# One stage of a four-stream decoder kernel: chunk loads, order of the MLP's matmuls, value heads and row maximum changed together

## The reference

```python
scores = jnp.einsum('bhid,bhjd->bhij', q, k) * scale
kerple = -p * jnp.log1p(a * dist[None])
combined = jnp.concatenate([attn_t, kerple_t], axis=-1)         # 16 scores, 16 kerple values per (i, j)
hdn = jax.nn.gelu(jnp.dot(combined, w1) + b1, approximate=False) # w1 is 32 x 32
refined = jnp.dot(hdn, w2) + b2                                  # w2 is 32 x 16
scores = scores + kerple[None] + refined
scores = jnp.where(causal[None, None], scores, -jnp.inf)
weights = jax.nn.softmax(scores, axis=-1)
out = jnp.einsum('bhij,bhjd->bhid', weights, v)
```

## Time and profile before

| what | value |
|---|---|
| runs | 5373.63, 5384.91, 5383.06 us |
| the profiled execution | 5373.67 us |
| its span, first to last instruction | 5371.9 us |
| mean granted TensorE clock | 0.918 |
| PE / PEld / DVE / ACT busy in the span | 4611.2 / 2081.7 / 2563.6 / 1934.2 us |
| second half of A in the second round | 1478 to 1763.2 us |

### The profile page before, as it was taken

How to read it: one execution, slowest core, us unless ns; L and a number is a source line. 1 busy time by engine, 2 the same in 40 slices (tenths; PEclk the granted TensorE clock), 3 DMA queues, 4 the chain that set the end, 5 groups by cost and what they waited for, 6 DMA issues and landing times.

```text
span 5371.9 us, 51967 instructions
## 1 busy us (share of the span) xinstructions
PE 4611.2 (86%) x18614; PEld 2081.7 (39%) x18714; DVE 2563.6 (48%) x5396; ACT 1934.2 (36%) x3234; POOL 308.7 (6%) x299
## 2 busy tenths in 40 slices
PE   5897888899788778889978877888997887788999
PEld 2333334345434333434533423342453342334345
DVE  4455635542345563554234566365423546535632
ACT  5542432331554243333155333333315533323320
POOL 1000130000000013000000002300000000230000
PEclk9998978999899898899989988899998998889999
DMA  6744003312374400331237440032213734004121
GB/s 235 155 101 83 14 1 73 59 63 73 106 137 93 83 14 4 81 48 68 68 112 140 84 83 14 27 69 37 74 62 126 140 71 83 14 32 81 19 83 57
DMA packets 173150, 398.65 MB, mean 74 GB/s; under 512 B 16164, under 2 KB 93988, under 8 KB 161828
## 3 DMA queue, kind: packets, MB, share of 16 engines
q1 hardware_dynamic: 172872, 395.08, 31.3%
HBM read 315.33 MB, written 79.69 MB: 74 GB/s over the span
## 4 chain that ended last, share of the span: by engine, by line
PE 66%; DVE 16%; DMA 8%; ACT 4%; issue 3%; SPq 2%; another core or an unknown queue 1%; POOLq 0%; DVEq 0%; ACTq 0%
PE ps L1020 9%; PE ps L510 6%; PE ps L1278 5%; DVE mx L640 5%; PE ps L1288 5%; PE ps L493 5%; PE ps L1038 4%; PE ps L436 4%; PE ps L1313 3%; DMA a_cmb<-scores_kerple 3%; PE ps L780 3%; PE ps L762 3%; PE ps L332 2%; DMA qparts<-QP 2%; ACT a_rot L1353 2%
## 5 line engine op out<-in xcount | busy, mean ns | idle before, releaser
L640 DVE TENSOR_REDUCE mx<-ps 128x1 f32<-128x512 f32 (+3 forms) x1280 | 770.2, 645 | 537.0 <-PE ps L441 260.6
L584 ACT ACTIVATE PT<-ps 128x1024 f32<-128x1024 f32 (+3 forms) x640 | 604.7, 958 | 522.4 <-PE ps L498 287.6
L436 PE MATMUL ps<-KS,QS 96*128 96x512 bf16 (+3 forms) x1280 | 488.2, 404 | 195.2 <-DMA QS<-qparts 116.9
L1020 PE MATMUL ps<-xnT,f_w 128*128 128x512 f32 x1088 | 488.8, 593 | 0.0
L493 PE MATMUL ps<-QS,KS 99*128 99x512 bf16 (+2 forms) x1280 | 425.5, 377 | 9.0 <-ACT QS L574 6.2
L1278 PE MATMUL ps<-a_cmb,w1A 128*128 128x512 f32 (+1 forms) x704 | 370.2, 610 | 48.8 <-DMA a_cmb<-scores_kerple 48.1
L510 PE MATMUL ps<-PT,VP 128*32 128x512 f32 (+3 forms) x2560 | 380.7, 581 | 3.3
L332 PE MATMUL ps<-mneg,identb 128*128 128x512 bf16 x856 | 214.4, 409 | 141.9 <-issue 50.1
L1118 DVE TENSOR_TENSOR f_tm<-f_si,ps 128x512 f32<-128x512 f32 x128 | 88.0, 687 | 503.2 <-ACT f_si L1070 503.1
L436 PEld LDWEIGHTS ps<-KS,QS 96*128 96x128 bf16 x1280 | 130.1, 102 | 486.3 <-DVE mx L640 278.1
L1070 ACT ACTIVATE f_si<-ps 128x512 f32<-128x512 f32 x136 | 80.8, 597 | 607.6 <-PE ps L1033 588.5
(11 more groups left out here) (245 smaller groups left out, 6576.1 us busy)
## 6 DMA issues: line engine op xcount, KB each, us to landing
f_w<-in_wF SPq DMA_DIRECT2D x136, 384.0 KB, 3.0
a_cmb<-scores_kerple SPq DMA_DIRECT2D x64, 512.0 KB, 10.7
a_cmb<-scores_kerple SPq DMA_DIRECT2D x64, 384.0 KB, 11.1
VP<-in_v_unit SPq DMA_DIRECT2D x12, 2048.0 KB, 10.5
KS<-kparts SPq DMA_DIRECT2D x96, 256.0 KB, 9.6
QS<-qparts SPq DMA_DIRECT2D x144, 128.0 KB, 5.2
scores_kerple<-a_Ss SPq DMA_DIRECT2D x16, 1024.0 KB, 6.2
a_cmb<-scores_kerple SPq DMA_DIRECT2D x64, 256.0 KB, 8.1
```

Of the source, the lines that this page charges most:

```text
L436: last = nc.tensor.matmul(o, m["QS"][0:KR, h, i * P:(i + 1) * P], m["KS"][0:KR, h, f:f + w], start=True, stop=plain)
L584: nc.scalar.activation(m["PT"][:, mp % 2, j % 2, :, 0:w], ps[:, b0:b0 + 2, 0:w], ACT.Exp, scale=HD ** -0.5).then_inc(g("exp"), 1)
L640: nc.vector.tensor_reduce(m["mx"][:, h % 2, i, f // BANK:f // BANK + 1], ps[:, k % 2, 0:w], AX.X, ALU.max, negate=True).then_inc(g("slot_f ...
L1020: last = nc.tensor.matmul(ps[:, 2 * v + e % 2, :], m["w"][:, e % NRING, (2 * v + k) * P:(2 * v + k + 1) * P], xnT[:, k, :], start=(k == 0) ...
```

## The change

Five edits, all in the first attention:

1. `load(c)`: the four `a_cmb` DMAs become two, one for each half f, each writing all 128 partitions. The source of each has the row group as its outermost dimension (4), then the 32 values.
2. The waits for the stores of row tiles 1, 2 and 3 stood before the first load of each tile (chunks 4, 8, 12); now all three stand before `load(1)`, which is before the mid-stage barrier.
3. TensorE's order: instead of up, down, up, down it is two ups, then the two downs of the pair before, one in each half of the array's columns.
4. `weighted`: for each pair of heads and each key tile j, first the even head (lower half of the columns), then the odd head, instead of all j of one head after another.
5. VectorE: the addition of the table and the row maximum are one operation per row, `tensor_tensor_reduce`, instead of an addition per row and one `tensor_reduce` per chunk.

```diff
@@ -1202,11 +1204,10 @@
 
             def load(c):
                 i, r, R, L = chunk(c)
-                rows = sk[i].rearrange("r (f g q) j -> g r f (q j)", f=2, g=4)
+                rows = sk[i].rearrange("r (f g q) j -> f g r (q j)", f=2, g=4)
                 part = slice(r * L, (r + R) * L)
-                for u in range(4):
-                    sp.dma_start(M2["cmb"][32 * u:32 * u + 32, c % 2, 
-                                 :, 0:R * L], rows[u, :, :, part]).then_inc(g(f"cmb{c % 2}"), 16)
+                for f in range(2):
+                    sp.dma_start(M2["cmb"][:, c % 2, f, 0:R * L], rows[f, :, :, part]).then_inc(g(f"cmb{c % 2}"), 16)
                 if c >= 4:
                     sp.wait_ge(g("tr"), TURNS_TO[c - 3])
                 rows = sk[i][0:AH].rearrange("h (g q) j -> g h (q j)", g=8)
@@ -1223,8 +1224,9 @@
                 sp.dma_start(sk[i][4 * hq:4 * hq + 4].rearrange("h p j -> p h j"),
                              M1["Ss"][:, 4 * sum(TRI_L[:i]):4 * sum(TRI_L[:i + 1])].rearrange("p (h l) -> p h l", h=4)).then_inc(g(f"out{i}"), 16)
             for c in range(1, NCHUNK):
-                if CHUNKS[c][1] == 0:
-                    sp.wait_ge(g(f"out{CHUNKS[c][0]}"), 4 * 16)
+                if c == 1:
+                    for i in range(1, NI):
+                        sp.wait_ge(g(f"out{i}"), 4 * 16)
                 if c >= 2:
                     sp.wait_ge(g("w1"), UNITS_TO[c - 1])
                 load(c)
@@ -1271,7 +1273,7 @@
                 c, f, q = A_UNITS[k]
                 i, _, _, L = chunk(c)
                 if k == UNITS_TO[c]:
-                    pe.wait_ge(g(f"cmb{c % 2}"), 16 * 4 * (c // 2 + 1))
+                    pe.wait_ge(g(f"cmb{c % 2}"), 16 * 2 * (c // 2 + 1))
                 if k >= 3:
                     pe.wait_ge(g("gelu"), k - 2)
                 R = SA_R[i]
@@ -1305,9 +1307,8 @@
 
             def weighted(i):
                 pe.wait_ge(g("pt_up"), TURNS_TO[TILE_END[i] + 1])
-                for h in range(AH):
-                    r, t = AW * (h % 2), h // 2
-                    for j in range(i + 1):
+                for t, j, e in itertools.product(range(AH // 2), range(i + 1), range(2)):
+                        h, r = 2 * t + e, AW * e
                         rhs = m["PT"][:, j, :, :].rearrange("p q (g h) -> p h g q", h=AH)[:, h]
                         o = ps[r:r + AW, 4 + t // 4, (t % 4) * P:(t % 4 + 1) * P].rearrange("p (g q) -> p g q", g=8)
                         last = nc.tensor.matmul(o, m["V"][:, j, h * AW:(h + 1) * AW], rhs, start=(j == 0), stop=(j == i), tile_position=(0, r))
@@ -1327,10 +1328,12 @@
             for s in range(NCHUNK + 3):
                 c = s - 2
                 if s < NCHUNK:
-                    for k in range(UNITS_TO[s], UNITS_TO[s + 1]):
-                        if k + 2 < len(A_UNITS):
-                            up(k + 2)
+                    for k in range(UNITS_TO[s], UNITS_TO[s + 1], 2):
+                        for e in (k + 2, k + 3):
+                            if e < len(A_UNITS):
+                                up(e)
                         down(k)
+                        down(k + 1)
                 if 0 <= c < NCHUNK:
                     turn(c, 0)
                 if s - 3 in TILE_END:
@@ -1427,12 +1430,12 @@
                         for q in range(q0, q0 + R):
                             row = m["fin"][:, slot, q * L:(q + 1) * L]
                             t0 = BACK - i * P - (r + q)
-                            last = nc.vector.tensor_tensor(row, row, biasA[:, t0:t0 + L], ALU.add)
+                            last = nc.vector.tensor_tensor_reduce(row, row, biasA[:, t0:t0 + L], 1.0, NEG, ALU.add, ALU.max,
+                                                                  m["nm"][:, slot, q:q + 1])
                         ch.link(last)
                     if s >= 2:
                         turned(s - 2, 1)
                     nm = m["nm"][:, slot, 0:CR]
-                    ch.link(nc.vector.tensor_reduce(nm, m["fin"][:, slot, 0:CR * L].rearrange("p (q l) -> p q l", q=CR), AX.X, ALU.max))
                     nc.vector.tensor_scalar(nm, nm, -1.0, None, ALU.mult).then_inc(g("negm"), 1)
                 if NCHUNK <= s < NCHUNK + 2:
                     turned(s - 2, 0)
```

More of the change, by code:

```diff
@@ L8 @@
+import itertools
 import numpy as np
```

## The result

| | before | after |
|---|---|---|
| median, four executions each | 5383.99 us | 5648.60 us |
| from to | 5373.63 to 5388.82 | 5634.32 to 5676.92 |
| after / before | | 1.050 [1.046, 1.054] |
| the profiled execution | 5373.67 | 5676.92 |
| mean granted TensorE clock | 0.918 | 0.880 |

The change makes the kernel 265 us slower. The forecast was +862 (6245); the direction and the place are right, the size is 3.3 times too large.

What follows compares the result with a forecast made beforehand. The prediction took DMA on four engines to bound stage A's second half: +216 us a round, +864 for four. 5373.7 + 864 = 6237.7; with the median 9.4 above the profiled execution, 6245, own range 5950 to 6400.

Steps and rivals of the forecast that it cites:

- Four engines: New a_cmb loads, source outermost dimension 4, run on four engines, assumed among a_fin's eight; 0.74 at 12.5 to 19 GB/s each.
- Bounds of the rate: Per engine in the new loads: 14.9 GB/s chosen, between 13.1 (+273 us a round) and 26.4 (+112).
- the term of 430 us for the loads: Second half of stage A: after chunk 0's load, 25.56 MB on four engines at 59.5 GB/s take 429.6 us a round.
- Rival 1: Four engines load undisturbed at 26.4 GB/s each: +112 us a round, 5495 us; chance 0.13.
- the signs that the prediction had named: Second half of A: DMA share 0.25 to 0.3, 50 to 70 GB/s, TensorE busy under half, clock below 0.93.
- No gap opens in between: Second half of A: each chunk's load is issued while the previous one still arrives, so loading never pauses.
- The chunk of 44 us: A row tile 3 chunk, 2.62 MB on four engines, takes 44 us to load; TensorE needs about 18.
- The tail and the clock: From the last landing to stage B: 64 us, plus 8 us (0 to 35) for a lower TensorE clock.
- Edit 2: Moved store waits delay chunk 1's load and the barrier: some 9 us a round, bounds 0 to 15.
- Edit 3: Second down of a pair is free: 40.6 us a round if TensorE sets the pace, here only 4.
- Edit 5: Combined addition and maximum on VectorE: 0 taken; saving 2.3 us or costing 1.3 in each of the last two chunks.
- Rival 2: New loads still spread over sixteen engines, TensorE sets the pace: -45 us a round, 5203 us; chance 0.09.

Runs made afterwards that it cites:

- e3_rmajor: After with the a_cmb partitions ordered value first and w1A's rows permuted to match, so the source's outermost dimension is 32: 5197.25 us.
- e8_two: After with each a_cmb load cut into two of 64 partitions, source outermost dimension 2: 6360.03 us.
- e10_eight: After with a_cmb partitions value first and each load cut into four by value, 32 partitions a load, source outermost dimension 8: 5312.37 us.
- e9_few_fin: After with most of a_fin not loaded from chunk 5 on and other data for chunks 1 to 4, so scores are wrong: 5590.64 us.
- e1_loads: Before with only the new two a_cmb loads per chunk and the store waits moved ahead of load(1): 5731.84 us.
- e7_waits: Before with only the store waits moved ahead of load(1) and the barrier: 5403.30 us.
- e5_max: Before with only addition and row maximum made one operation: 5367.29 us.
- e2_rest: After with the old four a_cmb loads per chunk, all other edits kept: 5361.75 us.
- e4_pairs: Before with only TensorE's order changed to two ups, then two downs: 5328.46 us.
- e11_four: After with a_cmb partitions value first and each load cut into eight by value, 16 partitions a load, source outermost dimension 4: 5720.69 us.

## Why the prediction was right in kind and wrong in size

**Four engines: right**, shown by the shares and by e3_rmajor and e8_two. That they are among `a_fin`'s eight is right too (0.52 with both in flight).

**The step that failed is "Bounds of the rate", and with it the term of 430 us for the loads.** It took 14.9 GB/s an engine "of the load with the most similar source and target". That row shows eight engines at little more than half of what eight moved in e10_eight, and I carried its rate to four. My own sentence beside it, that 119 GB/s for both eight and sixteen engines is a limit of what is shared, should have moved the choice towards 26.4. In after, windows of 3 us from 1552.77 on add up to 30.7 MB by the last `a_cmb` landing at 1853.7, in 301 us: 102 GB/s. Five sixths of it are the four's by the prediction's own bytes (26.2 of 31.5 MB), 85 GB/s or 21 each. With 85 for 59.5 GB/s the 25.56 MB take 301 us and not 430: -129 us a round, and that alone turns +216 into +87; measured are +75 and 6.7 at the barrier in the second round, and 66 a round in the medians. Rival 1's rate (26.4) errs nearly as far to the other side of 21 as 14.9 does, but in time it is closer: 5495 against 5649, since time goes with the inverse. The windows show three kinds of stretches below 26.4: starts at 59 to 67 GB/s (the partitions are the likely cause, not shown), `a_fin` beside (0.52 to 0.53 with 112 to 134 GB/s, 13 to 16 each; e9_few_fin), and ends and gaps in which two engines or none are at work. Of the signs that the prediction had named, the quarter share and the lower clock (0.80 over the half) came, but so did the sign against it, 90 GB/s and more at a quarter share (106), and TensorE was busy for 63% of the half, not for under half of it.

**"No gap opens in between" failed too**, though the total hides it. The chain of waits from 1700 to 1915 us of after names the loads for 40.8% of the time and TensorE's own rows for most of the rest; three of its pieces (start, us, what):

```profile
1701.59 8.59 PE ps L1314 x64
...
1716.83 40.01 DMA a_cmb<-scores_kerple
...
1805.90 47.79 DMA a_cmb<-scores_kerple
```

In e9_few_fin no byte moves from 1704.77 to 1708.77, just behind `weighted`. With two buffers a load waits for TensorE's ups, so TensorE's time is not free in this kernel. That this is why edits 3 to 5 took 83 us off e1_loads, 21 a round where I had 4, is argued, not shown.

**The chunk of 44 us** was near for row tile 3 (40.0 and 47.8 us above, each including what is queued ahead), and wrong for the sum: in row tile 2 two loads follow each other by 23 us (issued at 1662.94 and 1685.94) where 1.97 MB at 59.5 GB/s were to take 33.

**The tail and the clock.** From the last landing to stage B I had 64 + 8 us; it took 59.7 (1853.73 to 1913.47). The clock did fall to 0.50 while TensorE stood waiting for a load. But at the last landing TensorE had worked since 1830.82 with few pauses, on `weighted` of row tile 2 and the matmuls of chunk 14, and the clock stood at 1.00. It fell later, to between 0.50 and 0.84 from 1876.77 to 1891.77, and was 0.91 in the mean of the piece, where the same piece of before had 0.82 (1695.90 to 1763.22). So the 8 us for a lower clock are the second mis-sized term: nothing of it came.

**Edit 2: right.** I had 9 us a round within 0 to 15; the barrier comes 6.7 us later in round two and e7_waits measures 5.6 a round.

**Edit 3: right for TensorE.** Two downs now take 1.01 us together. TensorE of after in row tile 3 (start, us, line, form, count):

```profile
1765.31 0.64 PE L1290 MATMUL ps<-a_hid,w2A 128*64 128x512 f32 x1
1765.31 0.64 PE L1290 MATMUL ps<-xn,w2A 128*64 128x512 f32 x1
1765.79 0.59 PE L1290 MATMUL ps<-a_hid,w2A 128*64 128x512 f32 x1
1765.79 0.59 PE L1290 MATMUL ps<-xn,w2A 128*64 128x512 f32 x1
1766.31 1.98 PE L1280 MATMUL ps<-a_cmb,w1A 128*128 128x512 f32 x4
```

The pairs start in the same 10 ns. Two ups and two downs take 2.92 us (1765.31 to 1768.23) and took 4.12, 1.2 saved where I had 1.0. In after the loads hid most of it. With 16 engines on 128 partitions it can reach the time (e3_rmajor, 5197), though no run has those loads without edit 3.

**Edit 4: right** at 0. `weighted` of row tile 3, every matmul of it alternating, takes

```profile
1890.79 17.02 PE L1314 MATMUL ps<-a_PT,a_V 128*64 128x128 f32 x128 [0.78 <-DVE a_PT L1412]
```

where it took 16.57.

**Edit 5: right at 0 here**, inside its bounds: VectorE's new operation costs what the addition did, and its short partner 0.08 us and not 0.2.

```profile
1801.91 0.69 DVE L1433 CUSTOM_DVE_ANT_0 a_fin<-a_fin,biasA 128x512 f32<-128x512 f32 x1
1802.53 0.08 DVE L1433 DVE_READ_ACCUMULATOR2_ANT a_nm<- 128x1 f32 x1
```

Alone on before it is worth 3.4 us a round (e5_max), less than the 4.6 that 2.3 in each of the last two chunks would give.

**Rival 2** (sixteen engines, 5203) didn't happen. e3_rmajor, which gives the same edits sixteen engines, took 5197, but that it came so near is partly luck: rival 2 held 210 GB/s to be enough, and e2_rest, which has sixteen engines at that rate, took 5362, with 149 us of waits for `a_cmb`. e3_rmajor has 412 GB/s.

## What to carry to other kernels

Write down the outermost dimension of a load's source before counting the partitions it fills: it set how many of the sixteen engines worked here (2, 4, 8, 32 gave 2, 4, 8, 16), and reordering two dimensions, with the weights permuted to match, was worth 8% between after and e3_rmajor. A rate per engine read from a stretch in which eight engines work must not be carried to another number of engines; take the fastest and the slowest row per engine as the two ends, and remember that time goes with the inverse of the rate. When TensorE's work gets cheaper, look at the waits for loads first: in e4_pairs they grew by 90 us, and 56 of the 162 us hoped for were saved.

## What was not expected of the hardware

The same sixteen engines move 210 GB/s when a load writes 32 partitions and 412 when it writes 128 (e3_rmajor). Eight engines move 119 GB/s as 16 partitions each of 128, and 208 as 4 each of 32 (e10_eight): fewer partitions, nearly twice the rate. Four engines took 20 us of row tile 3's first load to reach 106 GB/s with `a_cmb` laid out in 32 partitions per row group (e9_few_fin, from rest), while loads of 16 partitions ran at 107 (e11_four, behind others). What sets these rates stays open.
